# Putting a projection's bias into the PSUM bank for half of the tiles only, and adding it in VectorE's eviction for the others

## What is computed

```python
h   = relu(layernorm(x))                      # 50000 x 256
msg = relu(h[src] + edge_attr)                # 25000 x 256, one row per edge
p   = msg @ W_fc.T + b_fc                     # 25000 x 256
scores = p @ Q.T                              # 4 heads
# softmax of the scores over the edges of each target node -> alpha
# mean of p over the edges of each target node, @ Wg.T + bg, softmax -> gate
pooled = segment_sum(alpha * p)               # per head
out = x + sigmoid(einsum(gate, pooled))       # 50000 x 256
```

## Time and profile before

| what | value |
|---|---|
| median of 3 runs | 657.8 us (657.22 to 658.36) |
| profiled execution, its own time | 653.36 us |
| its span, first to last instruction | 651.3 us |
| mean granted TensorE clock | 0.968 |
| TensorE matmul busy | 543.0 us (83%) |
| VectorE busy | 462.0 us (71%) |
| ScalarE busy | 416.3 us (64%) |
| GpSimd busy | 454.9 us (70%) |
| chain that ended last, by line | PE L803 22%, PE L895 22%, PE L788 5%, PE L800 3% |
| bias matmul L800 | 196 of them, 54.8 us busy |
| VectorE's eviction L1229 | 48 of them, 32.6 us busy |

### The profile page before, as it was taken

One profiled execution on the slowest core, in us unless ns is written; L12 is line 12 of the kernel. 1 busy time (PEld: TensorE's weight loads), 2 busy tenths in 40 slices (PEclk: granted clock), 3 DMA queues, 4 the chain that ended last, 5 costly groups with the idle time before them and its releaser, 6 DMA issues.

```text
span 651.3 us, 12707 instructions
## 1 busy us (share of the span) xinstructions
PE 543.0 (83%) x2670; PEld 439.9 (68%) x2671; DVE 462.0 (71%) x1607; ACT 416.3 (64%) x765; POOL 454.9 (70%) x342
## 2 busy tenths in 40 slices
PE   2799999999999999920899989878878876878775
PEld 2588888888887778810687768666666665656554
DVE  3986878998999998779776667555646555456454
ACT  1667778888897888723035556656665665666674
POOL 6777777777777777107045677787887878778784
PEclk9998999999999999975799999999999999899999
DMA  8566666766668899530289999999999999999999
GB/s 206 165 198 166 201 194 211 219 203 204 197 189 284 295 300 315 181 129 1 72 285 350 386 345 320 320 331 351 312 318 326 354 314 334 318 304 348 327 342 324
DMA packets 137275, 171.54 MB, mean 263 GB/s; under 512 B 10132, under 2 KB 123820, under 8 KB 137238
## 3 DMA queue, kind: packets, MB, share of 16 engines
q10 hardware_dynamic: 91344, 90.23, 42.3%
q1 hardware_dynamic: 33046, 42.70, 20.6%
q0 software_dynamic: 12848, 38.20, 18.5%
HBM read 111.50 MB, written 59.60 MB: 263 GB/s over the span
## 4 chain that ended last, share of the span: by engine, by line
PE 54%; DVE 15%; ACT 9%; issue 8%; POOL 4%; ACTq 3%; DVEq 3%; DMA 3%; POOLq 0%; SPq 0%
PE bank L803 22%; PE bank L895 22%; PE bank L788 5%; ACT arena L649 4%; POOL arena L516 4%; DVE spread L1406 4%; ACT bank L625 3%; PE bank L800 3%; DVE stats L1214 2%; ACTq L652 2%; DVEq L1410 1%; DMA p_keep<-in_x_dram,idx 1%; DVE arena L1220 1%; DVEq L1406 1%; DMA arena<-in_x_dram 1%
## 5 line engine op out<-in xcount | busy, mean ns | idle before, releaser
L895 PE MATMUL bank<-p_keep,spread 128*128 x1172 | 274.5, 388 | 54.3 <-DVE spread L1406 43.4
L895 PEld LDWEIGHTS bank<-p_keep,spread 128*128 128x128 f32 x1172 | 218.7, 192 | 110.9 <-issue 83.7
L1406 DVE TENSOR_SCALAR spread<-bank,rel,wgt 128x128 f32<-128x128 f32 x586 | 195.6, 403 | 131.4 <-PE bank L895 82.2
L516 POOL TENSOR_TENSOR arena<-arena 128x1024 f32<-128x1024 f32 x96 | 224.9, 2353 | 74.9 <-ACT arena L649 74.3
L803 PE MATMUL bank<-w_all,arena 128*128 128x264 f32 (+1 forms) x784 | 208.8, 389 | 0.0
L649 ACT ACTIVATE arena<-bank 128x1024 f32<-128x1024 f32 x97 | 99.3, 1023 | 139.7 <-PE bank L895 130.7
L479 POOL DMA_INDIRECT p_keep<-in_x_dram,idx x124 | 124.5, 1004 | 38.8 <-issue 31.4
L803 PEld LDWEIGHTS bank<-w_all,arena 128*128 128x128 f32 (+1 forms) x784 | 135.3, 192 | 15.8
L625 ACT ACTIVATE bank<-zero 128x1024 f32<-128x1024 f32 x98 | 100.5, 1026 | 3.0
L543 ACT ACTIVATE arena<-bank 128x256 f32<-128x256 f32 x196 | 74.2, 379 | 33.2 <-PE bank L788 32.6
L479 POOL DMA_INDIRECT arena<-in_x_dram,idx x72 | 73.5, 1020 | 23.1 <-issue 14.9
(11 more groups left out here) (248 smaller groups left out, 239.5 us busy)
## 6 DMA issues: line engine op xcount, KB each, us to landing
out_dram<-arena ACTq DMA_DIRECT2D x97, 512.0 KB, 4.4
arena<-in_x_dram ACTq DMA_DIRECT2D x73, 512.0 KB, 5.3
arena<-in_edge_attr_dram SPq DMA_DIRECT2D x48, 512.0 KB
arena<-in_x_dram POOLq DMA_DIRECT2D x24, 512.0 KB, 5.6
p_spill<-p_keep SPq DMA_DIRECT2D x16, 512.0 KB, 3.9
p_keep<-p_spill SPq DMA_DIRECT2D x16, 512.0 KB, 5.0
p_keep<-in_x_dram,idx POOLq DMA_INDIRECT x124, 2.8
arena<-in_x_dram,idx POOLq DMA_INDIRECT x72, 5.0
```

Source lines behind the costliest of these rows:

```text
L516: pool.tensor_tensor(yout[:, slot, :, :], yout[:, slot, :, :], xin[:, slot, :, :], ALU.add).then_inc(summed, 1)
L895: nc.tensor.matmul(places[:, bass.ds(place, T)], spread[:, k0 + k, :], p_rows[:, bass.ds(p_at, T)], start=False, stop=True, skip_group_che ...
L1406: v.tensor_scalar(spread[:, k, :], bank[:, 7, P:2 * P], rel[:, bass.ds(s0 + k, 1)], wgt[:, bass.ds(s0 + k, 1)], ALU.is_equal, ALU.mult).th ...
```

## The change

TensorE puts the bias into the bank only for the tiles that ScalarE evicts. For VectorE's tiles the first fp32 matmul opens the bank, and VectorE's two copies out of the bank become two additions that read the bank and `bias`. So that `bias` is still whole when they run, `finish_weights` keeps the remainders of the split in a new buffer `bias_rest` (128 x 264 fp32) instead of overwriting `bias`; it has as many instructions as before.

```diff
+        bias_rest = sb("bias_rest", [P, NT])
...
-                nc.tensor.matmul(bank[0:n, 2 + t % 4, 0:NT], part_rows[:, 0:n], bias_parts[:, :], start=True, stop=False)
+                biased = by_act(t // 2)
+                if biased:
+                    nc.tensor.matmul(bank[0:n, 2 + t % 4, 0:NT], part_rows[:, 0:n], bias_parts[:, :], start=True, stop=False)
                 pe.wait_ge(relu_done, t + 1)
                 for c in range(KD):
                     last = nc.tensor.matmul(bank[0:n, 2 + t % 4, 0:NT], msg_t[:, t % 4, c, 0:n], w_all[:, c, :],
-                                            start=False, stop=(c == KD - 1))
+                                            start=(c == 0 and not biased), stop=(c == KD - 1))
...
                 for first_row in (64, 96):
-                    rest = bias[first_row:P, :]
-                    then(v.tensor_tensor(rest, rest, bias_parts[first_row:P, :], ALU.subtract))
+                    rest, whole_ = bias_rest[first_row:P, :], (bias if first_row == 64 else bias_rest)[first_row:P, :]
+                    then(v.tensor_tensor(rest, whole_, bias_parts[first_row:P, :], ALU.subtract))
...
-                        v.tensor_copy(logits[:, t:t + 2, :], bank[:, b:b + 2, T:NT])
-                        v.tensor_copy(p_keep[:, slot:slot + 2, :], bank[:, b:b + 2, 0:T]).then_inc(p_by_dve, 1)
+                        v.tensor_tensor(logits[:, t:t + 2, :], bank[:, b:b + 2, T:NT],
+                                        bias[:, T:NT].unsqueeze(1).broadcast_to([P, 2, K]), ALU.add)
+                        v.tensor_tensor(p_keep[:, slot:slot + 2, :], bank[:, b:b + 2, 0:T],
+                                        bias[:, 0:T].unsqueeze(1).broadcast_to([P, 2, T]), ALU.add).then_inc(p_by_dve, 1)
...
-                    v.tensor_copy(logits[:, t, :], bank[:, b, T:NT])
-                    v.tensor_copy(logits[0:LAST, t + 1, :], bank[0:LAST, b + 1, T:NT])
-                    v.tensor_copy(p_keep[:, slot, :], bank[:, b, 0:T])
+                    v.tensor_tensor(logits[:, t, :], bank[:, b, T:NT], bias[:, T:NT], ALU.add)
+                    v.tensor_tensor(logits[0:LAST, t + 1, :], bank[0:LAST, b + 1, T:NT], bias[0:LAST, T:NT], ALU.add)
+                    v.tensor_tensor(p_keep[:, slot, :], bank[:, b, 0:T], bias[:, 0:T], ALU.add)
                     dve.wait_ge(padded, 1)
-                    v.tensor_copy(p_keep[0:LAST, slot + 1, :], bank[0:LAST, b + 1, 0:T]).then_inc(p_by_dve, 1)
+                    v.tensor_tensor(p_keep[0:LAST, slot + 1, :], bank[0:LAST, b + 1, 0:T], bias[0:LAST, 0:T], ALU.add
+                                    ).then_inc(p_by_dve, 1)
```

## The result

The kernel before took 656.7 us in the median of six runs (654.9 to 658.4), the changed one 650.0 (647.2 to 652.6): ratio 0.9899, with an interval of 0.9865 to 0.9933. That is 6.6 us less. The forecast had 2.5 us less. The profiled execution after took 647.2 us, with a span of 644.9.

What follows compares the result with a forecast made beforehand. Stage one was taken as bounded by GpSimd's gathers as a floor, nearly met by TensorE; 0.3 + 1.1 + 1.2 = 2.6 us, of which 2.5 taken, brought the median from 657.8 to 655.3 us, range 652.8 to 659.6.

Steps and rivals of the forecast that it cites:

- What bounds the kernel: Stage one: GpSimd's gathers, 1.31 to 1.34 us from start to start against TensorE's 1.22 us a tile, are a floor.
- The rival that has the full 10.8 us: Stage one: TensorE is the bound after all, 98 x 0.11 us count in full, giving 647.0 us; chance 0.04.
- GpSimd's one wait: Idle 1.52 us ahead of tile 136's gather, ring of gathered rows full; it goes, all later gathers start 1.2 us earlier.
- The sum: Terms for stage one: 0.3 + 1.1 + 1.2 = 2.6 us, of which 2.5 were taken.
- The rival that another wait for the ring takes its place: GpSimd, stage one: another wait for gathered-row places makes the 1.2 us 0; "no change" with the wait kept, 656.4, chance 0.2.
- The collisions: Gathers starting under VectorE's two-SBUF-input additions last longer, 10.4 us over stage one; the new additions were taken to cost GpSimd nothing.
- half a us to a us of chance: Allowance for chance in the gathers' collisions, within the forecast's own range of 653.3 to 656.8 us.
- The tail: Behind the last late gather, landed at 253.74: TensorE's backlog gives 0.3 us, ten VectorE tiles without bias matmul 1.1 us.
- The weights' load: First fp32 weights of a tile load beside a transpose instead of the bias matmul; taken as 0, at most 0.11 back.
- VectorE's additions: Evictions from copy to addition, 680 against 671 ns, taken as 0; rival that they hold up GpSimd: 661.3 us, chance 0.13.
- The scan of the earlier trace: Stage two's scan reading SBUF and a bank takes 0.55 us with GpSimd idle or busy: one SBUF input does not collide.
- Stages two and three move as a block: Behind stage one: nothing in these stages changes, so they only shift with its end and add nothing to the sum.

Runs made afterwards that it cites:

- experiments on the floor: Changed kernel without any bias matmul: 0.987; with gathers 4.6 us late: 1.0012. Kernel before with VectorE's bias matmuls doubled: 1.0089. Fewer gathers: before 0.9992, changed 0.9894.
- 8-column kernel: Changed kernel whose VectorE tiles get a bias matmul again, over 8 columns instead of 264; ratio to the kernel before 1.0001, stage one ends at 281.5 us.
- this part alone: Kernel before with all 196 bias matmuls, VectorE's evictions turned from copies into additions of a tile of zeros; ratio 1.0011 to the kernel before.
- longer program: Already fulfilled waits put ahead of TensorE's first work, 156 in the kernel before and 100 in the changed one; ratios to the kernel before 1.001 and 0.9913.

## Why the prediction was right and wrong

**What bounds the kernel: right.** GpSimd's uniform line of gathers is the floor under stage one, and a TensorE busy for all of 120 us was not the bound alone. The experiments on the floor show it from four sides. The rival that has the full 10.8 us, 647.0, came numerically nearer to the measured 650.0 than the forecast's 655.3 did, and it is refuted all the same: stage one gave 3.5.

**GpSimd's one wait: right.** In the four profiles before, the idle time ahead of tile 136's gather is 1.52 to 1.53 us; in the four after it is 0.30. The sum took 1.2 us. The rival that another wait for the ring takes its place did not happen on the whole: two of the four have one of 0.85 us ahead of tile 163, but so has one profile before and another a longer one, and all idle time between gathers went from 61.1 to 59.7 us by the means.

**The collisions: mis-sized.** The sum had nothing for the gathers' lengthening. It fell from 10.6 to 9.7 us by the means, 0.9 us, since other gathers start under VectorE's two-input additions. With the 1.4 us of idle time this makes the last gather start 2.4 us earlier (262.2 to 259.8), where 1.2 was summed. The text had named "half a us to a us of chance" here; its sign could not be foreseen, and whether these 0.9 us belong to the change or to the alignment of the moment stays open.

**The tail: right, a little large.** 0.3 + 1.1 = 1.4 us were summed behind the last late gather. From the start of the last gather to the end of the stage it was 17.8 us before and 16.7 after, by the means: 1.1 us. So stage one gave 2.4 + 1.1 = 3.5 us for a sum of 2.6.

**The weights' load: right in its size.** The tile became 0.11 us shorter in full. The 8-column kernel has the whole price left with 8 of the 264 columns; if the price is the matmul's own weight load, which fits, it goes away with it and does not come back elsewhere.

**VectorE's additions: right.** 678 against 680 ns, no gather lengthened, ratio 1.0011 for this part alone. The scan of the earlier trace rows was a good witness for another instruction of the same kind of inputs. By the rule that the Trainium skill (SBUF — State Buffer, section "SBUF: two separate sides") gives, a VectorE instruction with one SBUF input, outside the two-port modes, holds no port against GpSimd; the 102 gathers agree.

**"Stages two and three move as a block": this step failed.** Stage two did move as a block (37.4 to 37.9 us in every profile). The sum put both stages at nothing, because nothing in them changes. Stage three was shorter by 2.4 us in the profiles, more than twice the standard error, and the spans of the timed executions agree (2.6). This is most of what separates 6.3 us from the forecast 2.5: 1.0 more in stage one, 2.4 in stage three, and some 0.4 between the profiles and the timed runs. Its cause stays open. A longer program does not explain it, the granted clock does not, and single profiles speak against the time at which the stage starts and against the new buffer. What the forecast should have had is a term for it: a stage of 335 us moves by 3 us from one execution to the next of one kernel (334.6 to 337.8 us before), and single timed runs of the kernel before lie between 649.4 and 662.1 us. A range whose lower end lies 2.5 us below the forecast, against a base of three runs, leaves no room for that. The base alone was 1.1 us too high (657.8 against 656.7).

## What to carry to other kernels

When an engine is busy all the time, look whether another one, busier by its starts than by its busy time, runs an unbroken line beside it: GpSimd was "77% busy" with 1.3 us from start to start, and this line, not TensorE's 100%, set what 10.8 us less work were worth (3.5, and nothing for the next 10.8). To learn which of two close bounds holds, load the one and lift the other: at such a point this kernel gave 8.3 us upward and 3.5 downward for the same 98 matmuls. And give stages that a change doesn't touch a spread of their own in the range, taken from repeats where there are any; four profiles of each kernel were hardly enough to tell 2 us, while the spans of all timed executions, 26 and 136, told it.

## What was not expected of the hardware

A bf16 matmul of 8 columns between fp32 matmuls costs as much as one of 264 columns: 0.11 us, with the tile at 1.22 us in both cases and 1.11 without it. Making this matmul narrower gained nothing; leaving it out did.

A delay of 4.55 us put on GpSimd at 56 us of the stage, more than 90 us before the statistics of the changed kernel begin to wait for gathers (150.7, but for one wait of 0.17 us at 42.6), arrives at the end of the stage with 4.1 us. No lead absorbs it, because in that run GpSimd sits idle for no more than 0.31 us between any two later gathers and so has nothing to catch up with.

A gather that starts under an addition of two SBUF tiles is longer by what is left of the addition less 0.13 us (272 of 278 in eight profiles). In ten more cases it is the other way round: the gather starts at most 34 ns after the addition and takes its usual 0.95 to 0.96 us, and the addition is longer, 0.46 to 0.49 us instead of 0.41. Other gathers that start as close behind are the ones held up, so these starts alone do not tell which of the two gives way. An addition of a bank and one SBUF tile lengthened none of its 102 gathers.
